# Attention heads multiplied into the projection first, and a new order of work up to the first experts

## The reference

```python
# layer 0, convolution block
y = ln_last(x) -> einsum with inproj_w -> depthwise 3x3 conv                  # s0
s = the positions of y in four orders (rows, reversed, columns, reversed)
r = ln_last(s) @ ssm_in_w.T ; a, g = split(r) ; r = a * sigmoid(g)
r = depthwise conv of 3 along the positions ; r = r @ ssm_out_w.T
m = mean over the four orders of (nan_clean(r) + s), each put back in place
x1 = nan_clean(einsum(m, outproj_w)) + x
# layer 1, linear attention, 16 heads of 4 channels, xa = normalised x1
qkv = xa @ W_qkv.T ; k, v = layernorm(k), layernorm(v)                        # per head, ddof=1
kv  = einsum('bhnd,bhne->bhde', k, v) / 256 ; out = q @ kv
t2  = gelu((out + xa) @ W_proj.T) + xa + x1                                   # as the kernel has it
# layer 1, mixture of 8 experts, on xf = layernorm over channels of t2
w_dense = softmax over the 2 largest of xf @ Wg + bg, 0 elsewhere
result  = t2 + sum_e w_dense[:, e] * (gelu(xf @ W1[e] + b1[e]) @ W2[e] + b2[e])  # W1 64x256, W2 256x64
```

## Time and profile before

| | us |
|---|---|
| median of 3 runs (lowest, highest) | 90.0 (89.72, 90.81) |
| the profiled execution | 89.83 |
| its span, first to last instruction | 88.1 |

### The profile page before, as it was taken

One profiled execution on the slowest core, in us unless ns is written; L12 is line 12 of the kernel. 1 busy time (PEld: TensorE's weight loads), 2 busy tenths in 40 slices (PEclk: granted clock), 3 DMA queues, 4 the chain that ended last, 5 costly groups with the idle time before them and its releaser, 6 DMA issues.

```text
span 88.1 us, 1440 instructions
## 1 busy us (share of the span) xinstructions
PE 80.0 (91%) x428; PEld 52.1 (59%) x428; DVE 54.9 (62%) x168; ACT 56.0 (64%) x119; POOL 23.8 (27%) x50
## 2 busy tenths in 40 slices
PE   4999998989999998978996899999999979999950
PEld 1589874657484444464735388767886648556620
DVE  3006786179959954757867988894253968056370
ACT  4578715899488667657999248963990928800910
POOL 5649100002532233100205000600004504718600
PEclk9999999999999999999999999999999999999999
DMA  1999700000000000000000000000056200378001
GB/s 21 203 370 425 290 2 0 0 0 0 0 11 4 0 0 0 0 0 0 0 0 7 0 0 0 0 0 1 22 188 219 65 0 7 114 196 210 19 0 60
DMA packets 2647, 5.36 MB, mean 61 GB/s; under 512 B 432, under 2 KB 1104, under 8 KB 2512
## 3 DMA queue, kind: packets, MB, share of 16 engines
q1 hardware_dynamic: 2496, 5.19, 17.8%
q10 hardware_dynamic: 144, 0.09, 0.4%
HBM read 4.98 MB, written 0.29 MB: 60 GB/s over the span
## 4 chain that ended last, share of the span: by engine, by line
PE 75%; DVE 12%; issue 8%; POOL 1%; ACT 0%; DVEq 0%; POOLq 0%
PE psM L855 12%; PE psA L704 5%; PE psA L839 5%; PE psB L839 4%; PE psA L840 4%; PE psB L840 4%; PE psB L638 4%; PE psT L650 4%; PE psT L657 3%; PE psM L755 3%; PE psA L717 2%; PE psA L728 2%; PE psB L737 2%; PE psA L730 2%; PE psA L729 2%
## 5 line engine op out<-in xcount | busy, mean ns | idle before, releaser
L536 ACT ACTIVATE hs<-psA,early 128x512 f32<-128x512 f32 x16 | 11.1, 694 | 10.9 <-PE psA L840 8.8
L855 PE MATMUL psM<-hs,w_sb 128*64 128x256 f32 x128 | 14.9, 383 | 0.0
L855 PEld LDWEIGHTS psM<-hs,w_sb 128*64 128x64 f32 x128 | 8.8, 136 | 5.8 <-issue 1.4
L536 ACT ACTIVATE hs<-psB,early 128x512 f32<-128x512 f32 x16 | 11.1, 695 | 0.0
L1267 DVE SCALAR_TENSOR_TENSOR prod<-psM,early,wbc 128x256 f32<-128x256 f32 x16 | 7.0, 475 | 6.3 <-DMA wbc<-gate_mem 3.9
L638 PE MATMUL psB<-warm 128*128 128x512 bf16 x25 | 7.9, 449 | 1.1 <-DVE warm L969 1.1
L364 POOL TENSOR_TENSOR acc<-acc,prod 128x512 f32<-128x512 f32 x5 | 6.4, 1282 | 5.2 <-DVE prod L1267 5.0
L839 PE MATMUL psA<-xh,w_hl 128*128 128x512 f32 x16 | 6.9, 430 | 0.1
L839 PE MATMUL psB<-xh,w_hl 128*128 128x512 f32 x16 | 6.3, 395 | 0.0
L840 PE MATMUL psA<-xl,w_hl 128*128 128x512 f32 x16 | 6.3, 393 | 0.0
L840 PE MATMUL psB<-xl,w_hl 128*128 128x512 f32 x16 | 6.3, 392 | 0.0
(11 more groups left out here) (210 smaller groups left out, 183.3 us busy)
## 6 DMA issues: line engine op xcount, KB each, us to landing
wbc<-gate_mem SPq DMA_DIRECT2D x16, 128.0 KB, 3.1
w_nat<-in_w_dram SPq DMA_DIRECT2D x1, 1024.0 KB, 7.7
late<-in_late_dram SPq DMA_DIRECT2D x1, 616.0 KB, 5.6
w_sb<-in_w_dram SPq DMA_DIRECT2D x1, 512.0 KB, 8.5
ssm_in<-in_ssm_dram SPq DMA_DIRECT2D x1, 320.0 KB, 4.5
x_sb<-in_x_chan_dram SPq DMA_DIRECT2D x2, 128.0 KB, 2.5
out_dram<-fin SPq DMA_DIRECT2D x2, 128.0 KB, 2.3
early<-in_early_dram ACTq DMA_DIRECT2D x1, 89.5 KB, 2.7
```

Source lines behind the costliest of these rows:

```text
L536: nc.scalar.activation(hs[:, n % RING, :], hidden_bank(n), ACT.Gelu, bias=cols(V_B1 + n % (E * CK))).then_inc(S["h_ok"], 1)
L855: m = nc.tensor.matmul(psM[q * C:(q + 1) * C, bank, c0:c0 + L], w2_sb[:, s % (E * CK), :], hs[:, s % RING, q * L:(q + 1) * L], start=(k == ...
```

## The change

Six things change together; the rest of the diff is order.

1. Heads times projection first: instead of (heads x query + xa) x W_proj the kernel computes (heads x W_proj) x query and adds xa x W_proj in the same PSUM bank ahead of it (`projected_heads`, `heads_with_projection`, `projection_of_input`). `retrieval` and `with_query_input` go.
2. The head matrix takes two VectorE instructions. The values' scale is put into a third block of the key and value weights (`value_weights` on GpSimd, `weighted_values` on TensorE, `kv_bias_parts` 384 wide), the values' bias is a second matmul in `head_products`, and the keys' scale and bias with the mask are made as rows by `key_norm_diagonals`, `key_norm_rows` and `key_norm_copy`. `kv_scaled` becomes `values_scaled` and two `keys_scaled`.
3. The third centering works on x and on the cleaned output apart (`centered_input`, `centered_with_output`), so it doesn't wait for `residual`.
4. For pair 0, t2 is not added before the transposition: x1 + xa is multiplied by the identity into the token banks, and the gelu is added there by a second matmul (`residual_to_tokens`, `gelu_to_tokens`). t2 is made later, for the final sum. Pair 1 keeps its transposition.
5. Pair 0's reciprocal root is done on ScalarE (`first_token_rsqrt`), half of its normalised copies too (`second_half_copies`), and the transposition back, `token_high` and `token_low` go by halves.
6. `hidden` of expert 0 issues both matmuls with xh ahead of both with xl. `keep_clock` is called 3 times in all, with 7, 3 and 5 matmuls, instead of 9 times.

The core of the diff:

```diff
+            def value_weights():
+                pool.wait_ge(S["kvw_ok"], 1)
+                nc.gpsimd.tensor_tensor(kv_w[:, 2 * P:3 * P], kv_w[:, P:2 * P], vln_w, ALU.mult).then_inc(S["vvw_ok"], 1)
+                pool.wait_ge(S["kvb_ok"], 1)
+                nc.gpsimd.tensor_tensor(kv_b[:, 2 * P:3 * P], kv_b[:, P:2 * P], vln_w, ALU.mult).then_inc(S["vvw_ok"], 1)
...
+            def heads_with_projection(h):
+                act.wait_ge(S["hp_ps"], h + 1)
+                nc.scalar.copy(heads_proj[:, h, :], psT[:, h, L:L + P]).then_inc(S["hp_ok"], 1)
...
+            def first_token_rsqrt():
+                act.wait_ge(Q["t2_mv"][0], 1)
+                nc.scalar.activation(var_eps[:, 0, :], mv[:, 0, :, 1], ACT.Ln, bias=LN_EPS_TOKEN).then_inc(S["tln_ok"], 1)
+                act.wait_ge(S["tln_ok"], 1)
+                nc.scalar.activation(rstd4[:, 0, :], var_eps[:, 0, :], ACT.Exp, scale=-0.5).then_inc(Q["t2_rstd"][0], 1)
+
+            def second_half_copies():
+                act.wait_ge(S["lessm_ok"], 1)
+                for q in range(2):
+                    src = token_major(0, 1)[:, q * C:(q + 1) * C].unsqueeze(1).to_broadcast([P, 2, C])
+                    m = nc.scalar.activation(norm_d[:, 0, q * T + 1, :, :], src, ACT.Identity, bias=less_mean[:, q:q + 1],
+                                             scale=rstd4[:, 0, 2 + q:3 + q])
+                m.then_inc(S["norma_ok"], 1)
...
+            def centered_input(h):
+                pe.wait_ge(Q["c_norm"][h], 1)
+                pe.wait_ge(Q["t_lnv"][h], 2)
+                nc.tensor.matmul(psT[:, h, 0:L], center[:, :], x_sb[:, h, :], start=True, stop=False)
+
+            def centered_with_output(h):
+                pe.wait_ge(S["oclean_ok"], h + 1)
+                pe.wait_ge(S["center_c_ok"], 1)
+                nc.tensor.matmul(psT[:, h, 0:L], center_c[:, :], o_sb[:, h, :], start=False, stop=True)\
+                             .then_inc(Q["cen_ps"][h], 1)
...
+            def residual_to_tokens():
+                pe.wait_ge(S["x1xa_ok"], 1)
+                pe.wait_ge(S["hp_ok"], 1)
+                pe.wait_ge(S["heads_ok"], 1)
                 for t in range(T):
+                    nc.tensor.matmul(token_major(0, t), x1_xa[:, 0, t * P:(t + 1) * P], ident[:, :], start=True, stop=False)
+
+            def gelu_to_tokens():
+                pe.wait_ge(S["gelu_ok"], 1)
+                for t in range(T):
+                    m = nc.tensor.matmul(token_major(0, t), gelu_p[:, 0, t * P:(t + 1) * P], ident[:, :], start=False, stop=True)
+                m.then_inc(Q["t2T_ps"][0], 1)
...
+            def projection_of_input(h):
+                pe.wait_ge(Q["c_norm"][h], 2)
+                pe.wait_ge(S["query_ok"], h + 1)
+                nc.tensor.matmul(psM[:, h, 0:L], proj_w, xa_c[:, h, :], start=True, stop=False)
+
+            def projected_heads(h):
                 pe.wait_ge(S["heads_ok"], h + 1)
+                nc.tensor.matmul(psT[:, h, L:L + P], heads[:, h, :], proj_w, start=True, stop=True).then_inc(S["hp_ps"], 1)
+
+            def projection(h):
+                pe.wait_ge(S["hp_ok"], h + 1)
                 pe.wait_ge(S["query_ok"], h + 1)
+                nc.tensor.matmul(psM[:, h, 0:L], heads_proj[:, h, :], query[:, h, :], start=False, stop=True)\
+                             .then_inc(S["p_ps"], 1)
...
+                if e == 0:
+                    pe.wait_ge(S["xh_ok"], T * (h + 1))
+                    for c, w in ks:
+                        if c >= 4:
+                            pe.wait_ge(S["h_ok"], c - 3)
+                        nc.tensor.matmul(hidden_bank(c), w, xh[:, h, :], start=True, stop=False)
+                    pe.wait_ge(S["xl_ok"], T * (h + 1))
+                    for c, w in ks:
+                        nc.tensor.matmul(hidden_bank(c), w, xl[:, h, :], start=False, stop=True).then_inc(S["h_ps"], 1)
...
             def head_matrix(h):
                 dve.wait_ge(S["heads_ps"], h + 1)
+                dve.wait_ge(S["kln_ok"], 1)
+                nc.vector.tensor_tensor(heads1[:, h, :], psA[:, h, L:L + P], kln_rows[:, 0, :], ALU.mult).then_inc(S["h1_ok"], 1)
                 dve.wait_ge(S["h1_ok"], h + 1)
+                nc.vector.scalar_tensor_tensor(out=heads[:, h, :], in0=kln_rows[:, 1, :], scalar=psA[:, h, L + P:L + P + 1],
+                                               in1=heads1[:, h, :], op0=ALU.mult, op1=ALU.add).then_inc(S["heads_ok"], 1)
```

400 lines of the change are left out of this document (214 added, 186 removed).

## The result

The changed kernel takes 91.56 us (median of 20 runs, 90.50 to 92.16) where the kernel before takes 90.38 (20 runs, 89.72 to 91.37): ratio 1.0109, 95% interval 1.008 to 1.0138. The ratio leaves out the executions that took over 1.5% more than the fastest of their kernel, and the medians above, of all 20, give 1.013. The changed kernel is about 1% slower; 88.4 us was forecast, with a range to 90.7. The profiled execution took 91.63 us with a span of 89.9, against 89.83 and 88.1 before.

The account below looks back on a forecast made before the run. TensorE's pace was taken to bound most stretches, but in the attention the chain to the first expert matmul. Terms -0.9, -0.43 and -0.2 sum to -1.5 us, span 86.6; forecast 88.4 us, range 87.0 to 90.7.

Parts of the forecast that it names:

- Up to xa_c(0): Stretch before pair 0's centered output: wider kv_bias_parts and moved weights hidden by full TensorE; costed at nothing.
- The square sums and the scaling: Pair 0's square and head matrix: head_rstd(0) +0.7 us later, shorter head matrix pays most back, heads ready +0.15.
- Heads times projection: From pair 0's heads to its gelu: 1.6 us instead of 2.33, gelu start near 42.85 us, -0.6 so far.
- Residual into the token banks: Pair 0's gelu to statistics: VectorE add of about 0.5 us goes, matmuls replacing transposes +0.25; -0.8 so far.
- Reciprocal root on ScalarE: Pair 0's reciprocal root moves from GpSimd to two ScalarE activations, ending at 46.5 us; -0.95 so far.
- ScalarE up to the experts: From the root to hidden(0), ScalarE works without a hole for 3.4 us; experts start at 49.95 us, -0.9.
- TensorE in the experts: projection(1) now before hidden(0), -0.43 us; first expert 0.93 instead of 1.17 us, -0.2.
- Rival 1: Gates through memory come too late for the experts' output products; nearly all gain lost, 89.7 us; chance 0.14.
- Rival 2: TensorE's clock falls with fewer keep_clock fillers before the experts; put at 91.8 us; chance 0.10.
- Rival 3: More gained than counted: VectorE's slow 4-element sum parts from GpSimd's adding, ScalarE steps short; 87.6 us; chance 0.20.

Follow-up runs that it names:

- before_wide_bias: The kernel before with only kv_bias_parts widened from 256 to 384 columns, the third block zeros set by GpSimd; ratio to the kernel before 1.006.
- after_spread: The changed kernel with the seven kv_bias_parts instructions split into three pieces between the gated_u steps; ratio to the kernel before 1.002.
- after_best: The changed kernel with kv_bias_parts in three pieces, 14 VectorE memsets, and pair 0's chain moved ahead in the queues; ratio to the kernel before 1.000.
- before_less17: The kernel before with 19 already covered VectorE waits left out (its expectation counts 17); ratio to the kernel before 1.008.
- after_rstd_first: The changed kernel with head_rstd(0) ahead of center_squares(2,1) and weighted_values(0) ahead of variance(2,1); ratio to the kernel before 1.008.
- before_pad: The kernel before with 14 one-column memsets added early on VectorE; ratio to the kernel before 1.005.
- before_less_waits: The kernel before with 13 already covered VectorE waits left out; ratio to the kernel before 1.005.

## Why the prediction was wrong

**Up to xa_c(0)** failed, by +0.59 us. The sentence was "the wider kv_bias_parts (384 instead of 256 columns) and the moved weights are hidden by the same full TensorE. If that cover fails, raster and column start later and everything shifts with them." The moved weights were hidden: GpSimd's two products took 0.56 and 0.45 us and the six weights ended at 19.54, 0.1 ahead of raster(0,0). The wide instructions were not hidden. Full TensorE (no idle time in the earlier trace rows) was no evidence of slack: it said that each product came just in time, and VectorE had stood in front of one of them. before_wide_bias shows 0.41 us for the width alone, after_spread gives 0.51 of the 0.59 back.

**The square sums and the scaling**: +0.7 and -0.55, so +0.15 at the heads, were forecast; +0.75 was measured (heads ready 7.92 us behind xa_c(0), before 7.17). ScalarE's square of pair 1 and head_rstd(0) began 0.2 to 0.3 later than I had it, since the bad-value mask of the output came late from GpSimd, behind attention_residual(0). The rest is a wait that I had left out: values_scaled also needs weighted_values, which stood on TensorE behind variance(2,1), and this behind that square.

```profile
38.79 0.38 ACT L420 ACTIVATE cen_sq<-psT 128x256 f32<-128x256 f32 x1 [0.69 <-PE psT L709]
39.07 0.30 ACT L521 ACTIVATE ss_ln<-ss 128x128 f32<-128x128 f32 x1
```
```profile
40.70 0.42 DVE L1282 TENSOR_TENSOR kv_n<-psT,rinv 128x256 f32<-128x256 f32 x1 [2.07 <-PE psT L856]
```

**Heads times projection**: -0.6 was forecast at the gelu, 0 measured (9.55 us behind xa_c(0) both times). The new path itself was costed right: 1.63 us from the heads to the gelu, 1.6 forecast. It started 0.75 later than before, which took the whole gain. after_best shows that an earlier start would have met pair 1's keys and values on TensorE and the squares of pair 1, which I had ending "at about 42.7" and which ended 0.6 later in the same count.

**Residual into the token banks**: the gelu to the statistics took 1.27 us instead of 1.47, so -0.2 where about -0.25 was forecast from these steps alone. The two plain products took 0.71 from start to end where the two transpositions of before took 0.44: a factor of 1.6.

```profile
45.49 0.49 PE L731 MATMUL psT<-ident,gelu_p 128*128 128x128 f32 x2
45.81 0.39 PE L731 MATMUL psA<-ident,gelu_p 128*128 128x128 f32 x2
```

TensorE: Matmul & The Clock Gate (the Trainium skill, Terms) has FP32 transpose mode four times as fast; the measurement decides here, for less than two.

**Reciprocal root on ScalarE** and **ScalarE up to the experts** were right in size: two activations of 0.19 and 0.20, then table, copies and halves of xh without a hole, 3.6 us from the root to hidden(0) against 3.45. The root ended 13.0 us behind xa_c(0) where the forecast's count has 12.6; the gelu had started 0.6 behind its forecast. In sum hidden(0) came 0.33 us earlier against xa_c(0) instead of 0.9.

```profile
48.20 0.20 ACT L571 ACTIVATE rstd<-var_eps 128x4 f32<-128x4 f32 x1
48.43 1.28 ACT L636 ACT_TABLE_LOAD   x1
...
51.52 0.37 ACT L557 CAST xh<-psT 128x256 fp32r<-128x256 f32 x1
```

**TensorE in the experts**: -0.44 measured, -0.63 forecast. Expert 0 took 1.05 us (52.04 to 53.09), between the 1.17 of before and the 0.93 that I had counted; the rest isn't located.

**Behind the experts** the prediction had nothing. Rival 1 had the place, gates that go through memory, but counted pair 0, where there was a margin of over a us (gates ready at 58.85 us, gate_rows(0) at 60.70). Of pair 1 it only says that the rows "move with TensorE", although it quotes the wait of 3.43 us, and the slack there was near nought. It had no mechanism for a longer transfer, and I gave it 0.14. It cost 1.07 us (0.75 in the write, 0.30 in the read-back) and is, with the 0.59 of kv_bias_parts, more than the whole difference. Rival 2 did not happen: the record of the granted clock stays at 1.00 from 6.51 us to the end, and the eight fillers behind 31 us took 0.25 to 0.27 us each, not the 0.45 of the start. Rival 3 did not either: VectorE's sum of 4 elements took 1.07 us as before.

The steps that missed add up: 0.59 up to xa_c(0), 0.57 up to hidden(0), 0.19 in the first experts and 1.07 behind them are 2.4 us, which turn the forecast -1.5 into +0.9, the difference of the two traces from the first ssm product on.

Why a fetch lengthens the write is shown in part. The write goes out as 16 packets of 1 KB, each followed by one of 4 bytes. In the changed kernel 15 of the 16 start 0.82 to 1.02 us behind the issue, as before. The last one starts at 1.26, where the fetch (0.71 to 1.26) ends, and its 4 bytes at 1.30 instead of 1.06. So it is in all eight executions with such a fetch: one packet alone is late, and it starts within 0.01 us of the fetch's end (before_less17 1.21, after_rstd_first 1.31). That fits one of the 16 DMA engines being held by the fetch; the trace doesn't name the engine. This is 0.1 to 0.3 us of the delay. The rest is that the read-back starts 0.8 to 1.0 us behind the last 4 bytes instead of 0.4. DMA: Bandwidth & Descriptors (the Trainium skill, Queues, rings and completion order) states that a transfer's semaphore is a strongly ordered write, which lands only after every earlier write of the same DMA engine, across its queues. CRC Debugging (the Trainium skill, Comparing the Two Runs) names queue 14 as the one that refills instructions. By that rule the write's semaphore would also wait until the 8 KB of the fetch have landed, and a fetch that is over before the write would cost nothing. The eight executions with a fetch 0.7 to 1.0 us behind the issue and the one with a fetch 0.65 ahead of it agree with this; the landing of the 8 KB itself is in no view.

## What to carry to other kernels

An engine that is never idle shows that its inputs come in time, not that they come early: before work is called hidden behind it, look for the slack of the instruction that releases it. Where a small transfer through memory stands on the path with no slack, its time can depend on what else is in the DMA queues at that moment, and here VectorE's instruction fetch moved with the number of instructions and waits ahead of it; give such a transfer some cover, or check the queues in a window of 1 us around it. When a chain for one half of the data is shortened, write down what of the other half stands in the same queues: here the 0.4 and 0.7 us won by pair 0 in two kernels were lost again behind pair 1's work on TensorE and ScalarE.

## What the hardware did that I had not expected

- Leaving 19 waits out of the kernel before, all of them already fulfilled, moved an 8 KB instruction fetch by 4.1 us against the gate write, into it, and made the last stage 1.1 us longer and the time 0.8% (0.5 to 1.2%); leaving out 13 of them, without that collision, also measured 0.5% slower. 14 memsets of one column brought the changed kernel from 1.011 to 0.996 and 1.000.
- The fetch follows VectorE's own instructions. The trace records VectorE's semaphore waits among them, and counted with these the fetch starts between VectorE's record 188 and 197 in all 18 executions. Pair 1's sum of maxima is record 205 in before_pad (fetch 10.4 us ahead of the write's issue), 191 or 192 in the old order and 193 in the new one with memsets (3.3 to 3.6 ahead), 183 in before_less_waits (0.65 ahead), and 179 in the changed kernel, its variants without memsets on VectorE and before_less17 (0.7 to 1.0 behind). Leaving out 13 and 19 waits took only 8 and 12 records away. The count in the expectations, one for each wait beyond the first of an instruction, puts before_less_waits level with the changed kernel, and their fetches lay 1.4 us apart: it is why that expectation missed.
- The same 16 KB write took 1.42 or 1.43 us in the ten profiled executions with no fetch in it, and 2.05 to 2.37 in the eight with one. The read-back behind it, by contrast, took from 3.5 to 4.1 us to the first use of its first two transfers of 128 KB, in kernels that differ in nothing near it; that is open, and so are about 0.5% of time in before_less_waits and before_pad. Write and read-back together took 4.92 to 5.56 us without a fetch in the write and 5.64 to 6.20 with one.
- The 7 fillers at the start took 3.17 us in both traces, but the first centering behind them took 0.69 us in one and 1.06 in the other. The granted clock reads 1.00 in both only because there is no record of it yet: the first record starts at 4.40 and at 6.51 us, and over 18 executions each us by which it is later costs half a us at the first ssm product.
